# A graph network on one core: who issues late loads, how many buffers the messages have, and how many partitions a matrix is loaded with

## The reference, cut to what matters

```python
# layer 0, attention with 4 heads of 64
e = leaky_relu(a_src[src] + a_dst[dst], 0.2)
ex = exp(e - segment_max(e, dst)[dst])
out = segment_sum(h[src] * ex / segment_sum(ex, dst)[dst], dst)
# layer 1, messages with filters made from 20 attributes of each edge
filt = silu(edge_attr @ Wf1 + bf1) @ Wf2 + bf2
agg = segment_sum(h[dst] * filt, src)
# layer 2, two weighted sums, one along and one against the edges
a_in = segment_sum(feat_in[src] * iw[:, None], dst)
a_out = segment_sum(feat_out[dst] * ow[:, None], src)
# layer 3: a small perceptron and two more attentions with one head of 32
```

## Time and profile before

| | us |
|---|---|
| runs | 7676.36, 7680.75, 7712.44 |
| the profiled execution | 7726.66, its span 7724.9 |
| PE busy | 5179.0 (67%) |
| DVE busy | 4741.9 (61%) |
| POOL busy | 3063.2 (40%) |
| ACT busy | 2201.6 (28%) |
| mean granted clock of PE | 0.794 |

### The profile page before, as it was taken

How to read it: one execution, slowest core, us unless ns; L and a number is a source line. 1 busy time by engine, 2 the same in 40 slices (tenths; PEclk the granted TensorE clock), 3 DMA queues, 4 the chain that set the end, 5 groups by cost and what they waited for, 6 DMA issues and landing times.

```text
span 7724.9 us, 88068 instructions
## 1 busy us (share of the span) xinstructions
PE 5179.0 (67%) x23224; PEld 3468.1 (45%) x23225; DVE 4741.9 (61%) x6614; ACT 2201.6 (28%) x4590; POOL 3063.2 (40%) x4180
## 2 busy tenths in 40 slices
PE   8512344599955599933488856666666899994838
PEld 4311232488832277733133325555555644483213
DVE  9862122375522288879599977877777600027987
ACT  6411011143311155322255532222221400013524
POOL 0377777507777700089300007776676000000000
PEclk7555666799965599965799977777777899995968
DMA  9970111149976633197422226666666123304675
GB/s 235 250 160 11 31 43 37 58 138 294 295 249 216 217 130 129 76 277 221 142 67 80 70 94 199 200 199 193 198 199 166 40 118 132 132 17 140 194 203 148
DMA packets 717764, 1158.60 MB, mean 150 GB/s; under 512 B 273349, under 2 KB 487003, under 8 KB 702994
## 3 DMA queue, kind: packets, MB, share of 16 engines
q1 hardware_dynamic: 374010, 608.16, 27.7%
q10 hardware_dynamic: 228664, 291.39, 11.2%
q0 software_dynamic: 114784, 255.38, 10.6%
HBM read 670.62 MB, written 483.97 MB: 149 GB/s over the span
## 4 chain that ended last, share of the span: by engine, by line
PE 30%; DVE 19%; issue 17%; DMA 9%; another core or an unknown queue 8%; POOL 8%; SPq 7%; ACT 1%; ACTq 0%; DVEq 0%; POOLq 0%
PE psall L1502 10%; PE psall L1475 8%; DVE arena L2172 7%; SPq L683 5%; POOL slots_by_src L953 5%; DMA arena<-weights_out 3%; PE psall L1635 3%; POOL arena L964 2%; DMA arena<-weights_in 2%; PE psall L1568 2%; DVE arena L2367 2%; DMA arena<-table_x,arena 2%; DVE arena L2165 2%; DVE arena L2224 2%
## 5 line engine op out<-in xcount | busy, mean ns | idle before, releaser
L964 POOL DMA_INDIRECT arena<-table_x,arena x856 | 958.4, 1120 | 1245.7 <-DMA arena<-slots_by_src 929.5
L953 POOL DMA_INDIRECT slots_by_src<-arena,pos_s x806 | 991.2, 1230 | 843.5 <-PE psall L1502 581.9
L1545 PE MATMUL psall<-arena 128*65 128x312 f32 (+3 forms) x3000 | 949.9, 441 | 296.1 <-DVE arena L2172 296.0
L1475 PE MATMUL psall<-shared_w,arena 128*128 128x256 f32 x3264 | 856.2, 419 | 336.6 <-DVE arena L2084 269.0
L925 POOL DMA_INDIRECT slots_by_block_pair<-arena x806 | 796.8, 989 | 552.0 <-DVE arena L1949 301.9
L1502 PE MATMUL psall<-arena 128*128 128x250 f32 x2880 | 792.3, 424 | 321.8 <-issue 277.4
L1121 ACT ACTIVATE arena<-psall 128x250 f32<-128x250 f32 (+2 forms) x1002 | 327.0, 367 | 1910.9 <-PE psall L1580 660.8
L1475 PEld LDWEIGHTS psall<-shared_w,arena 128*128 128x128 f32 x3264 | 665.2, 210 | 456.9 <-DVE arena L2084 266.4
L1502 PEld LDWEIGHTS psall<-arena 128*128 128x128 f32 x2880 | 565.8, 208 | 548.8 <-issue 496.8
L1568 PE MATMUL psall<-arena 128*125 128x256 f32 x1712 | 573.9, 508 | 344.4 <-DVE arena L2224 224.4
L2084 DVE TENSOR_TENSOR arena<-psall,shared_w 128x512 f32<-128x512 f32 x408 | 280.3, 691 | 833.6 <-remote 566.6
(11 more groups left out here) (323 smaller groups left out, 7452.9 us busy)
## 6 DMA issues: line engine op xcount, KB each, us to landing
arena<-counts SPq DMA_DIRECT2D x375, 312.5 KB, 3.4
arena<-slots_by_src SPq DMA_DIRECT2D x107, 1040.0 KB
filters<-arena ACTq DMA_DIRECT2D x204, 520.0 KB
slots_by_src<-shared_on SPq DMA_DIRECT2D x8, 9230.0 KB
arena<-filters SPq DMA_DIRECT2D x138, 520.0 KB
counts<-arena ACTq DMA_DIRECT2D x125, 312.5 KB
weights_in<-arena ACTq DMA_DIRECT2D x125, 312.5 KB
arena<-counts ACTq DMA_DIRECT2D x25, 1562.5 KB
```

The costliest lines, as they stand in the source:

```text
L953: G.indirect_dma_start(slots_s, bass.IndirectOffsetOnAxis(ap=pos_s[:, c:c + 1], axis=0), ring_s[:, g % SLOTS, c % TG, :], None).then_inc(r ...
L964: G.indirect_dma_start(hg[:, f % 2, j, :], None, t_x1, bass.IndirectOffsetOnAxis(ap=pay_s[:, f % 2, j, S_IDX:S_IDX + 1].bitcast(I32), axis ...
L1475: last = MM(to, hidT[:, sl % 2, c, j * LANES:(j + 1) * LANES], wf2[:, c, :], start=(c == 0), stop=(c == 1))
L1545: last = MM(ps[gat_bank(n, wn, h_, c)][0:F + 1, 0:z - a], rows, g["e1"][:, q % RE, a:z], start=(b == 0), stop=(b == NT - 1))
```

## The change

- `pay_s` and `hg` get three buffers each (`EDGE_RING`), with their semaphores; records and gathers of step f wait for step f - 3. Three loads of records are issued ahead of the store of the rows instead of two. The one-hots `oh` and those of the weights keep two.
- The 120 steps of weights are spread over the turns 0 to 107 by `weight_steps`: one in each, and two in each ninth turn (12 in all). The turns end at 110.
- POOL loads the filters of the groups from 154 on itself, as it does the first 64; SP loads 64 to 153.
- `weights_out` has 25 x 128 rows, and its stores, and the loads of both matrices into `a_ring`, use 128 partitions. PE still reads 125.
- In attention of layer 0 DVE multiplies two heads by the counts in one instruction (`AT_ONCE`), and `e1` has six buffers. The other attentions stay at one and five.
- One semaphore (`as_more`) is merged with another.

```diff
+EDGE_RING = 3
...
-        weights_out = dram("weights_out", (N, NT * LANES))
+        weights_out = dram("weights_out", (NT * LANES, NT * LANES))
...
-        v_out = weights_out.rearrange("(d p) s -> p d s", p=P)
+        v_out = weights_out.rearrange("(d p) s -> p d s", p=LANES)
...
-        a_ring = [view(o_, P, WI[1][0]) for o_ in o_ring_a]
+        a_ring = [view(o_, LANES, WI[1][0]) for o_ in o_ring_a]
...
-        pay_in, feat_in = ([sem(f"{n}{s}") for s in range(2)] for n in ("pay_in", "feat_in"))
+        pay_in, feat_in = ([sem(f"{n}{s}") for s in range(EDGE_RING)] for n in ("pay_in", "feat_in"))
+
+        def weight_steps(i):
+
+            return range(min(W_STEPS, W_STEPS * i // (F_STEPS + 1)), min(W_STEPS, W_STEPS * (i + 1) // (F_STEPS + 1)))
...
+        def by_pool(g):
+
+            return g < S2_EARLY or g >= S2_LATE
...
-            for g in range(S2_EARLY, S2_G):
+            for g in range(S2_EARLY, S2_LATE):
                 sp.wait_ge(ringed[g % SLOTS], 16 * ring_count(g - SLOTS))
                 sp.dma_start(ring_s[:, g % SLOTS, :, :], vf[:, TG * g:TG * (g + 1), :]).then_inc(fst[g % SLOTS], 16)
...
             def edge_load(f):
-                if f >= 2:
-                    sp.wait_ge(s["e_onehot"], f - 1)
-                    sp.wait_ge(s["e_msg"], f - 1)
-                sp.dma_start(pay_s[:, f % 2, :, :], vs[:, F_T * f:F_T * (f + 1), :]).then_inc(pay_in[f % 2], 16)
-
-            edge_load(0)
-            edge_load(1)
+                if f >= EDGE_RING:
+                    sp.wait_ge(s["e_onehot"], f - EDGE_RING + 1)
+                    sp.wait_ge(s["e_msg"], f - EDGE_RING + 1)
+                sp.dma_start(pay_s[f % EDGE_RING], vs[:, F_T * f:F_T * (f + 1), :]).then_inc(pay_in[f % EDGE_RING], 16)
+
+            for f in range(EDGE_RING):
+                edge_load(f)
...
-                sp.dma_start(a_ring[q % 3][:, 0:n], (v_in, v_out)[way][0:P, b, a0:a0 + n]).then_inc(ctl[q % 3], 16)
+                sp.dma_start(a_ring[q % 3][:, 0:n], (v_in, v_out)[way][:, b, a0:a0 + n]).then_inc(ctl[q % 3], 16)
...
             for g in range(S2_G):
-                if g < S2_EARLY:
-                    if g + 2 < S2_EARLY:
-                        early_load(g + 2)
+                if g == S2_LATE:
+
+                    pool.wait_ge(s["cb_mm"], 1 + T1)
+                    for k in (g, g + 1):
+                        own_load(k)
+                if by_pool(g):
+                    if g + 2 < (S2_EARLY if g < S2_EARLY else S2_G):
+                        own_load(g + 2)
                     pool.wait_ge(ringed[g % SLOTS], 16 * (1 + (ring_count(g - SLOTS) if g >= SLOTS else 0)))
                 else:
                     pool.wait_ge(fst[g % SLOTS], 16 * (FILTERS + (g - S2_EARLY) // SLOTS + 1))
-                if g == S2_LATE:
-
-                    pool.wait_ge(s["cb_mm"], 1 + T1)
...
+                r = f % EDGE_RING
+                pool.wait_ge(pay_in[r], 16 * (f // EDGE_RING + 1))
                 for j in range(F_T):
-                    if f >= 2 and j % TS_G == 0:
-                        pool.wait_ge(s["e_sum"], F_G * (f - 2) + j // TS_G + 1)
...
+                    if f >= EDGE_RING and j % TS_G == 0:
+                        pool.wait_ge(s["e_sum"], F_G * (f - EDGE_RING) + j // TS_G + 1)
...
-                              stage_out[0:P, PAIRS * (g % 3):PAIRS * (g % 3 + 1), :]).then_inc(st_w[g % 3], 16)
+                              stage_out[:, PAIRS * (g % 3):PAIRS * (g % 3 + 1), :]).then_inc(st_w[g % 3], 16)
...
-            for i in range(max(W_STEPS + 1, F_STEPS + AHEAD)):
-                if 0 <= i - AHEAD < F_STEPS:
+            for i in range(F_STEPS + AHEAD):
+                if i >= AHEAD:
                     edge_sums(i - AHEAD)
-                if 1 <= i <= W_STEPS:
-                    weight_sums(i - 1)
+                for n in weight_steps(i - 1) if i else ():
+                    weight_sums(n)
...
                 def counted(q):
-                    a = g["e1"][:, q % RE, :]
+
+                    a = g["e1"][:, q % g["RE"]:q % g["RE"] + g["AT_ONCE"], :]
                     wait_counts(dve, f"gat{n}", q // g["H"])
-                    dve.wait_ge(s["g_exp"], g_steps[n] + q + 1)
-                    V.scalar_tensor_tensor(a, a, 2.0, g["ct"][:, q // g["H"] % g["NCT"], :], ALU.min, ALU.mult)\
-                        .then_inc(s["g_mul"], 1)
+                    dve.wait_ge(s["g_exp"], g_steps[n] + q + g["AT_ONCE"])
+                    times = g["ct"][:, q // g["H"] % g["NCT"], :].unsqueeze(1).to_broadcast([LANES, g["AT_ONCE"], WD])
+                    V.scalar_tensor_tensor(a, a, 2.0, times, ALU.min, ALU.mult).then_inc(s["g_mul"], g["AT_ONCE"])
 
                 for q in range(STEPS[n] + 2):
                     if q < STEPS[n]:
                         scores(q)
-                    if q >= 2:
+                    if q >= 2 and q % g["AT_ONCE"] == g["AT_ONCE"] - 1 and g["AT_ONCE"] == 2:
+                        counted(q - 3)
+                    if q >= 2 and g["AT_ONCE"] == 1:
                         counted(q - 2)
...
-            for i in range(max(W_STEPS, F_STEPS + AHEAD + 1)):
+            for i in range(F_STEPS + AHEAD + 1):
                 f = i - AHEAD
                 if 0 <= f < F_STEPS:
                     messages(f)
                 if 0 <= f - 1 < F_STEPS:
                     adds(f - 1)
-                if i < W_STEPS:
-                    weight_onehots(i)
-                if 0 <= f + 1 < F_STEPS:
+                for n in weight_steps(i):
+                    weight_onehots(n)
+                    if n == weight_steps(i)[0] and 0 <= f + 1 < F_STEPS:
+                        edge_onehots(f + 1)
+                    weighed(n)
+                if not weight_steps(i) and 0 <= f + 1 < F_STEPS:
                     edge_onehots(f + 1)
-                if i < W_STEPS:
-                    weighed(i)
```

More of the change, by code:

```diff
@@ L561, in gnn_kernel @@
         GROUPS = NB // PAIRS
+        def by_pool(g):
+            return g < S2_EARLY or g >= S2_LATE
         def ring_done(sl):
-            return 16 * sum((k < S2_EARLY) + min(TG, EC - TG * k) for k in range(sl, S2_G, SLOTS))
+            return 16 * sum(by_pool(k) + min(TG, EC - TG * k) for k in range(sl, S2_G, SLOTS))
         def ring_count(g):
-            return sum((k < S2_EARLY) + min(TG, EC - TG * k) for k in range(g % SLOTS, g + 1, SLOTS))
+            return sum(by_pool(k) + min(TG, EC - TG * k) for k in range(g % SLOTS, g + 1, SLOTS))
         def scores_of(h):
@@ L821, in _ @@
             sp.dma_start(ends_w, d_last).then_inc(s["tab_in"], 16)
-            for f in range(2, F_STEPS):
+            for f in range(EDGE_RING, F_STEPS):
                 edge_load(f)
@@ L1182, in scores @@
                     one = asd[:, b, h_:h_ + 1] if n == 0 else h3[:, b, G3 + 1:G3 + 2]
[L1183 removed]
+                    A(g["e1"][:, q % g["RE"], :], g["e1"][:, q % g["RE"], :], ACT.Exp, bias=one).then_inc(s["g_exp"], 1)
                 def sums_out(q):
```

68 lines of the change are left out of this document (35 added, 33 removed).

## The result

The changed kernel takes 7620.77 us in the median of six runs (7574.34 to 7641.84), the kernel before 7702.58 in six (7676.36 to 7718.66). The ratio is 0.989 with a 95% interval of 0.986 to 0.993: faster by 1.1%, where 3.7% was forecast, and above my range.

A forecast was written before the change was run, and what follows sets the result against it. DVE was taken to bound layer 0's attention, a ring the edges' stage, few DMA engines' loads the dense sums, SP's filter loads the gap. 68 + 17 + 141 + 58 = 284 us; 7680.75 - 284 = 7397 us, range 7310 to 7500.

The forecast's parts named there:

- part 1: Ahead of layer 0's attention: late filter loads moved from SP to POOL start the first score earlier; 74 - 6 = 68 us.
- part 2: Layer 0's attention: two heads' products in one DVE instruction, 250 instead of 500; 17 us, bounds nothing and 33.
- part 3: Edges' stage: rings of three and spread weights; 85 us from shorter steps and 56 at the end, 141 us.
- part 4: Sums by the dense weights: loads over 128 partitions keep PE busy; 58 us, bounds 0 and 58; stores elsewhere nothing.
- my 1265 us: Edges' stage: DVE's time after the change, 1128.5 + 61 + 24 + 52 us, 85 less than now.
- the 52 us that I had kept: Edges' stage: half of DVE's 103.6 us of waits for PE, expected to remain; bounds nothing and all of it.
- Rival (b): Edges' stage: DVE and PE with two one-hot buffers each are the limit, not the ring; 7543 us, chance 0.12.
- My 6 us for VectorE giving way in attention: Layer 0's attention: 99 POOL issues delay DVE by 0.06 us each, 6 us off the gain of 74.
- Rival (a): Layer 0's attention: DVE gives way to POOL's 99 issues, so 68 us becomes -22; 7487 us, chance 0.10.
- (c): Edges' stage: POOL's floor of 1196 us is reached, 210 us gained there; 7328 us, chance 0.10.
- (d): Sums by the dense weights: loads of 128 partitions come no sooner, 58 us lost; 7455 us, chance 0.05.
- (e): Edges' stage: with three loads and 24 gathers in flight features land later, slower than before; 8063 us, chance 0.03.

The follow-up runs named there:

- b0: The kernel before, unaltered, profiled on another chip than the first runs: 6879.22 us in the profile.
- a0: The changed kernel, unaltered, on another chip than the first runs: 6559.77 us against 6886.93 for the kernel before, ratio 0.952.
- e4: The changed kernel with the ring back at two and one weights' step a turn: ratio 0.952 of the kernel before.
- p1: The kernel before with only the late filter loads moved to GpSimd's queue: 6647.05 us, ratio 0.967 of the kernel before.

## Why the prediction failed, point by point

| us | forecast | chip A | chips B to F |
|---|---|---|---|
| part 1, gap ahead of attention | -74 | -73 | -225 (b0 to a0) |
| part 2, attention | -17 | -18 | -19 |
| last score to first gather | 0 | +1 | +88 (a0) |
| part 3, first to last message | -85 | +104 | -40 |
| of it, waits of the double turns and the next ones | +24 | +267 | +78 |
| part 3, tail | -56 | -53 | -60 |
| part 4, sums by the dense weights | -58 | -61 | -60 |

The row of first to last message is not part three alone on B to F: from e4 to a0, where only part three differs, the stage grows by 17 us, and the rest comes with the stores of part four. On A the two were not separated. On A the rest of the 152 us between the two profiles is 51 us ahead of the maxima, in stages the change does not touch. I put them down to chance, as the six runs spread over 67 us; b0, p1 and a0 begin the maxima within 8 us of one another.

**The step that failed** is in part 3: "In such a step the second pair of one-hots waits for PE's sums of the step before ... so some 2 us each, 24 us." I saw one wait of two, and took TensorE's mean work of a step (12.5 us) less VectorE's (10.65) for its length. But each is a chain that starts over with the product of its turn: product, edges' sums, weights' sums, one-hots. And a double turn brings two such waits, its own and that of the next turn, which I had not counted. On B to F the second is the costly one, as VectorE has only its additions to do ahead of the one-hots: 6.0 us each, and 0.4 us for the one that I had put at 2. On A both are long, 12.6 and 8.9 us, since TensorE ended up to 17 us after its records. Cost of a pair on A, waits and all: 29.28 + 19.06 - 2 x 10.53 - 5.06 = 22.2 us a pair, 267 us for twelve. On B to F 15.86 + 16.74 - 21.06 - 5.06 = 6.5 us, 78 in all. With A's 267 put in the place of 24, my 1265 us become 1508; measured were 1454.5. The difference of 53 is the other half of TensorE's waits, the 52 us that I had kept and that did not come: the normal turns run at VectorE's 10.53.

The chain could have been written out from the program. Of the length on A the rows held only a hint: 40.4 us of "issue" ahead of the weights' matmuls and 120.1 ahead of the edges'. Rival (b) named "PE's 1.5 us per step lost without a named cause". I counted that as an average instead of asking what a wait costs that ends only when TensorE has finished. Why TensorE is so late on A stays open.

**Part 1** came out as forecast on A, by the steps given: terms issued right after ACT's copy, score 18 us later. My 6 us for VectorE giving way in attention did not show: the products take 1454 ns. The size is A's alone, 225 us from b0 to a0, since the number of loads in SyncE's way depends on GpSimd's lag.

**Rival (a)**, VectorE gives way to GpSimd, is false on every chip; what happens is its reverse. I had written that if GpSimd were shut out of all of attention, the gathers would come 140 us late. On B to F it is shut out for 326 to 491 of some 733 us in ten profiles, and they come 10 to 92 us late. On A 62 scatters were left and none was shut out (2162 ns in the mean).

The Trainium skill, page "SBUF — State Buffer", section "Who interferes with whom", says that of a contending pair the second to issue blocks until the first has finished. The durations of 3.1 us under the maxima fit. A scatter that waits through 461 us of VectorE's 2.93 us pairs, some 157 of them, does not: each pair is over after 2.93 us, and it is not let in between them. It was let in at VectorE's first pause, in ten cases of ten.

**Part 2** by its steps (1.37 us start to start, 18 us). **Part 4** too; its loads were no bound at 128 partitions, TensorE busy 532.88 of 535 us. Its stores, costed at nothing "beside other work", gave some 60 us on B to F, by exclusion (e4 against b0 and p1).
Rivals (b) to (e): (b) has the right pair of engines, but its normal turns would have stayed at 12.74. (c) put the stage at GpSimd's 1196 us; with the weights first it comes near, at 1222 to 1226. (d) is false by the sums' 535 us, (e) by the 1.7 us of waits ahead of the product.

## What to carry to other kernels

Where work is bunched into some turns of a pipeline, write out the chain of the bunched turn, and of the turn behind it, from its first instruction; averages over turns say nothing of it. If its second piece needs a buffer that another engine frees in the same turn, let that engine free it before it turns to the fresh data. And price a queue's detour by the lag that fills it: on another chip of the same kind the lag, and so the gain, was three times as large.

## What the runs showed of the hardware

- The first runs of the same program were 12% slower than those on five other chips (7703 against 6871 to 6896 us). Their traces show hundreds of register instructions of TensorE's sequencer at 0.7 us where the others have none (251 us in sum over 0.2 us, less than the 820 lost), a granted clock of 0.794 in the profiled execution against 0.865 (b0), and VectorE's durations the same to the nanosecond (1752 and 1752 in L2263). Whether that is the chip or something else about those runs cannot be told from them. A change that leans on how fast an engine finishes can be worth 1% on one and 5% on the other.
- GpSimd can be locked out by VectorE for 326 to 491 us in one instruction: under gapless pairs of 1250 elements a scatter took 2.5 us or hundreds, under single products of 625, as gapless, 1.19 in the mean. The long ones ended in VectorE's first pause of over 1 us.
- With stores of 320 KB from 128 partitions instead of 312.5 KB from 125, a stage in which they were no one's wait was some 60 us shorter (no run changed them alone).
- TensorE's records can end long before its work does: 17.5 us in the double turn on A, by the semaphore that counts the matmuls; 0.04 us in a0.
